# Causal attention core: looks at the heads spread over twelve of sixteen steps, hyperbolic heads three steps apart

## The reference, cut to what matters

```python
def _sdpa(q, k, v, scale):
    scores = jnp.einsum('bhtd,bhsd->bhts', q, k) * scale + _causal_bias(...)
    return jnp.einsum('bhts,bhsd->bhtd', jax.nn.softmax(scores, axis=-1), v)

def _hyp_attn(q, k, v, curv):
    tq = jnp.sqrt(1.0 / curv + jnp.sum(q * q, axis=-1, keepdims=True))
    tk = jnp.sqrt(1.0 / curv + jnp.sum(k * k, axis=-1, keepdims=True))
    inner = jnp.einsum('bhtd,bhsd->bhts', q, k) - tq * jnp.swapaxes(tk, -1, -2)
    arg = jnp.maximum(-curv * inner, 1.0 + 1e-07)
    dis = jnp.sqrt(1.0 / curv) * jnp.arccosh(arg)
    scores = 1.0 / (eps + dis) + _causal_bias(...)
    return jnp.einsum('bhts,bhsd->bhtd', jax.nn.softmax(scores, axis=-1), v)
```

## Time and profile before

| | us |
|---|---|
| three runs | 5957.14, 5960.48, 5983.22 (median 5960.48) |
| the profiled execution | 5973.35 |
| its span, from the first to the last instruction | 5971.3 |
| busy over the span: TensorE, VectorE, ScalarE, GpSimd | 4632.2 (78%), 3844.7 (64%), 2507.9 (42%), 597.5 (10%) |
| the core "g", from about 2490 to about 3680 | some 1190 |
| mean granted TensorE clock over the span | 0.854 |

### The profile page before, as it was taken

One profiled execution on the slowest core, in us unless ns is written; L12 is line 12 of the kernel. 1 busy time (PEld: TensorE's weight loads), 2 busy tenths in 40 slices (PEclk: granted clock), 3 DMA queues, 4 the chain that ended last, 5 costly groups with the idle time before them and its releaser, 6 DMA issues. The chain is left out here.

```text
span 5971.3 us, 101861 instructions
## 1 busy us (share of the span) xinstructions
PE 4632.2 (78%) x27583; PEld 3020.9 (51%) x27583; DVE 3844.7 (64%) x9327; ACT 2507.9 (42%) x5760; POOL 597.5 (10%) x928
## 2 busy tenths in 40 slices
PE   6999978850029888587787786777799899789888
PEld 5667657640015555355555554555455555444444
DVE  3444433348878878777777665555677777477776
ACT  1222224347533333377777774222366666400000
POOL 0000000000000000100000000111111111122221
PEclk9999989975569989777777777888799999899999
DMA  2111113348974444332222222555433333211110
GB/s 65 52 54 52 50 53 144 144 169 253 355 274 125 127 130 123 87 75 69 69 69 69 71 72 69 157 154 154 105 93 85 88 94 91 77 45 46 49 50 27
DMA packets 379998, 617.03 MB, mean 103 GB/s; under 512 B 43190, under 2 KB 310004, under 8 KB 379892
## 3 DMA queue, kind: packets, MB, share of 16 engines
q1 hardware_dynamic: 367572, 614.35, 35.1%
q0 software_dynamic: 12320, 1.40, 0.2%
HBM read 345.02 MB, written 269.21 MB: 103 GB/s over the span
## 5 line engine op out<-in xcount | busy, mean ns | idle before, releaser
L1645 DVE TENSOR_REDUCE e_neg<-ps 91x1 f32<-91x273 f32 x1536 | 571.9, 427 | 137.4 <-PE ps L1466 130.0
L1578 ACT ACTIVATE e_probT<-ps 91x273 f32<-91x273 f32 x1536 | 491.7, 393 | 292.9 <-PE ps L1466 292.2
L1193 PE MATMUL ps<-k_downT,f_o 128*91 128x256 f32 x1152 | 260.1, 385 | 453.6 <-DVE f_o L1101 453.4
L2320 PE MATMUL ps<-m_we,m_xT 128*128 128x512 f32 x1104 | 521.6, 621 | 0.0
L1193 PEld LDWEIGHTS ps<-k_downT,f_o 128*91 128x91 f32 x1152 | 183.0, 161 | 522.4 <-issue 454.6
L1464 PE MATMUL ps<-c_mask_kq,c_identb 91*91 91x91 bf16 x1536 | 325.8, 243 | 104.4 <-ACT g_probT L1578 79.4
L1466 PE MATMUL ps<-e_k,e_q 96*91 96x273 bf16 x1536 | 344.0, 307 | 64.9 <-DMA e_k<-s_parts 28.8
L2254 DVE SCALAR_TENSOR_TENSOR m_acc<-ps,m_weight,m_acc 128x256 f32<-128x256 f32 x552 | 261.7, 481 | 173.6 <-PE ps L2320 163.7
L1466 PE MATMUL ps<-g_q,g_k 102*91 102x273 bf16 (+5 forms) x1536 | 331.0, 296 | 49.1 <-DVEq L1651 48.5
L2320 PEld LDWEIGHTS ps<-m_we,m_xT 128*128 128x128 f32 x1104 | 211.4, 198 | 223.3 <-issue 208.9
L1466 PE MATMUL ps<-e_q,e_k 128*91 128x273 bf16 x1536 | 286.7, 291 | 38.3 <-DMA e_q<-e_shift 36.4
(11 more groups left out here) (303 smaller groups left out, 10057.6 us busy)
## 6 DMA issues: line engine op xcount, KB each, us to landing
s_gate<-b_gu SPq DMA_DIRECT2D x32, 819.0 KB
s_up<-b_gu SPq DMA_DIRECT2D x32, 819.0 KB
c_g<-s_gate SPq DMA_DIRECT2D x32, 819.0 KB, 7.0
s_gated<-c_g SPq DMA_DIRECT2D x32, 819.0 KB
d_g<-s_gated SPq DMA_DIRECT2D x32, 819.0 KB, 10.4
d_u<-s_up SPq DMA_DIRECT2D x32, 819.0 KB
s_o<-d_o SPq DMA_DIRECT2D x32, 819.0 KB
f_o<-s_o SPq DMA_DIRECT2D x32, 819.0 KB
```

Of the source, the lines that this page charges most:

```text
L1193: last = nc.tensor.matmul(ps[0:R, t // 2, (t % 2) * D:(t % 2 + 1) * D], o[:, u, k, t * R:(t + 1) * R], downT[:, k, :], start=(k == 0), sto ...
L1578: nc.scalar.activation(probT[0:R, p % 8, b, :], src, ACT.Exp, scale=float(HD) ** 0.5 if kinds[h] == COS else 1.0)\
L1645: last = nc.vector.tensor_reduce(neg[:, u, t, h:h + 1], src, AX.X, ALU.max, negate=True)
L2320: last = nc.tensor.matmul(ps[0:R, EBANK[m % 4], :], xT[:, u, k, t * R:(t + 1) * R], we[:, k, 2 * p:2 * p + 2, :].rearrange("p e d -> p (e ...
```

## The change

In the core "g" the steps of the looks are given by a table. Before, ten looks stood at steps -11 to -2, hyperbolic and SDPA heads in turn (6, 0, 7, 1, 8, 2, 9, 3, 4, 5). Now they stand from -15 to -4: hyperbolic heads 8, 9, 6, 7 at -15, -12, -9, -6 and SDPA heads 0 to 5 at -11, -10, -8, -7, -5, -4. Root, sum and score keep their distance from the look. The negation moves from step 0 (p = 0) to step -1 (p = 15), the shift's turn from step 1 to step 0. Since heads are no longer looked at in the order of their numbers, the counts that the waits compare with go by the place in the order (`z`). The extra dimensions are loaded with each half for its own two hyperbolic heads.

```diff
-        LOADS = {0: 2 * len(RUNS) + (2 if hd > HD else 0), 1: 2 * len(RUNS)}
+        LOADS = 2 * len(RUNS) + (2 if hd > HD else 0)
...
-        first = -11 if n_hyp else -13
-        look_order = [h for pair in zip(HYPS, SDPAS) for h in pair] + SDPAS[n_hyp:]
-        look_step = {h: first + x for x, h in enumerate(look_order)}
+        if n_hyp:
+            look_step = {8: -15, 9: -12, 6: -9, 7: -6, 0: -11, 1: -10, 2: -8, 3: -7, 4: -5, 5: -4}
+        else:
+            look_step = {h: h - 13 for h in range(H)}
+        look_order = sorted(look_step, key=look_step.get)
         look = {place(step): h for h, step in look_step.items()}
+        looked_hyps = [h for h in look_order if h in HYPS]
...
-            NEGATE = place(look_step[HYPS[-1]] + SCORE + 1)
-            shifts = [(look_step[HYPS[-1]] + SCORE + 2, 0, MAXED)]
+            last_hyp = max(look_step[h] for h in HYPS)
+            NEGATE = place(last_hyp + SCORE + 1)
+            shifts = [(last_hyp + SCORE + 2, 0, MAXED)]
...
-                    if hd > HD and half == 0:
-                        sp.dma_start(dst[SLOTS * HD:rows, u, HYPS[0]:HYPS[0] + n_hyp], extra_dram[n, x])\
+                    if hd > HD:
+                        own = slice(max(HYPS[0], heads.start), min(HYPS[-1] + 1, heads.stop))
+                        sp.dma_start(dst[SLOTS * HD:rows, u, own],
+                                     extra_dram[n, x, :, own.start - HYPS[0]:own.stop - HYPS[0]])\
                             .then_inc(qk_loaded[u][half], 16)
...
-                    ways = 4 + max([g for g in back_step if back_step[g] - H < shifts[x][0]], default=-1)
+                    ways = 4 + max([g for g in back_step if back_step[g] - H <= shifts[x][0]], default=-1)
                     pe.wait_ge(S["out"].sem, S["out"].at((n[0], n[1] - 1), ways - 3))
...
-                for a, h in enumerate(HYPS):
+                for h in looked_hyps:
+                    a, z = HYPS.index(h), looked_hyps.index(h)
                     if (when, p) == place(look_step[h] + ROOT):
-                        act.wait_ge(S["hu"].sem, S["hu"].at(n, a + 1))
+                        act.wait_ge(S["hu"].sem, S["hu"].at(n, z + 1))
```

More of the change, by code:

```diff
@@ L1502, in step @@
                         if h == [x for x in look_order if x // HALF == half][0]:
-                            pe.wait_ge(qk_loaded[u][half], 16 * LOADS[half] * (i + 1))
+                            pe.wait_ge(qk_loaded[u][half], 16 * LOADS * (i + 1))
                     for which in (("max", "raw") if kinds[h] == HYP else ("max",)):
@@ L1585, in step @@
                     nc.scalar.copy(oT[:, g % 2], ps[:, 6, 0:T]).then_inc(S["oT"].sem, 1)
[L1586 removed]
+                for h in looked_hyps:
+                    a, z = HYPS.index(h), looked_hyps.index(h)
                     if (when, p) == place(look_step[h] + ROOT):
[L1588 removed]
+                        act.wait_ge(S["hu"].sem, S["hu"].at(n, z + 1))
                         nc.scalar.activation(hu[:, a], hu[:, a], ACT.Ln).then_inc(S["hl"].sem, 1)
[L1590 removed]
+                        act.wait_ge(S["hl"].sem, S["hl"].at(n, z + 1))
                         nc.scalar.activation(hu[:, a], hu[:, a], ACT.Exp, scale=0.5).then_inc(S["root"].sem, 1)
                     if (when, p) == place(look_step[h] + SCORE):
[L1593 removed]
+                        act.wait_ge(S["z"].sem, S["z"].at(n, z + 1))
                         nc.scalar.activation(hw[:, u, a], hw[:, u, a], ACT.Ln, bias=one[:]).then_inc(S["l1"].sem, 1)
[L1595 removed]
+                        act.wait_ge(S["l1"].sem, S["l1"].at(n, z + 1))
                         nc.scalar.activation(hw[:, u, a], hw[:, u, a], ACT.Ln, bias=eps6[:],
                                              scale=root_ic[:, a:a + 1]).then_inc(S["l2"].sem, 1)
[L1598 removed]
+                        act.wait_ge(S["l2"].sem, S["l2"].at(n, z + 1))
                         nc.scalar.activation(hw[:, u, a], hw[:, u, a], ACT.Exp, scale=-1.0)\
@@ L1626, in step @@
                         dve.wait_ge(S["s"].sem, S["s"].at(n, y + 1))
-                        dve.wait_ge(S["score"].sem, S["score"].at(n, a + 1))
+                        dve.wait_ge(S["score"].sem, S["score"].at(n, looked_hyps.index(ORDER[p]) + 1))
                         d = hw[:, u, a, b * T:(b + 1) * T]
@@ L1633, in step @@
                     a = HYPS.index(h) if kinds[h] == HYP else None
+                    z = looked_hyps.index(h) if kinds[h] == HYP else None
                     if a is not None:
@@ L1649, in step @@
                         else:
-                            dve.wait_ge(S["top"].sem, S["top"].at(n, a * NT + (1 if b == 0 else NT)))
+                            dve.wait_ge(S["top"].sem, S["top"].at(n, z * NT + (1 if b == 0 else NT)))
                             dve.sem_inc(S["looked"].sem, 1)
@@ L1660, in step @@
                                 .then_inc(S["looked"].sem, 1)
-                        dve.wait_ge(S["w"].sem, S["w"].at(n, a + 1))
+                        dve.wait_ge(S["w"].sem, S["w"].at(n, z + 1))
                         dve.wait_ge(S["looked"].sem, S["looked"].at(n, y + 1))
@@ L1665, in step @@
                             .then_inc(S["wc"].sem, 1)
-                        dve.wait_ge(S["z"].sem, S["z"].at(n, a + 1 - n_hyp))
-                        dve.wait_ge(S["wc"].sem, S["wc"].at(n, a + 1))
+                        dve.wait_ge(S["z"].sem, S["z"].at((n[0], n[1] - 1), z + 1))
+                        dve.wait_ge(S["wc"].sem, S["wc"].at(n, z + 1))
                         nc.vector.scalar_tensor_tensor(out=hu[:, a], in0=hw[:, u, a], scalar=2.0,
@@ L1671, in step @@
                             .then_inc(S["hu"].sem, 1)
-                for a, h in enumerate(HYPS):
+                for h in looked_hyps:
+                    a, z = HYPS.index(h), looked_hyps.index(h)
                     if (when, p) == place(look_step[h] + SUM):
-                        dve.wait_ge(S["root"].sem, S["root"].at(n, a + 1))
+                        dve.wait_ge(S["root"].sem, S["root"].at(n, z + 1))
                         nc.vector.tensor_tensor(hw[:, u, a], hw[:, u, a], hu[:, a], ALU.add).then_inc(S["z"].sem, 1)
```

4 lines of the change are left out of this document (removed).

## The result

The changed kernel takes 6199.52 us (median of 4 runs, 6181.94 to 6210.76); the kernel before 5971.85 (4 runs, 5957.14 to 5989.06). The ratio is 1.0377, 95% interval 1.0334 to 1.0421: slower, by some 225 us. The forecast was 6093 with an upper end of 6145. The direction was right, and the loss was 1.7 times the 133 us that I had worked out.

A forecast was written before the change was run, and what follows sets the result against it. No engine is full; waits in the fixed order set 36.4 us a batch. Walked 21.0 + 12.8 + 5.4 = 39.2, clock +1.3: 40.5; 31 periods +127, start +6, from the 5960.48 median: 6093 us, range 6020 to 6145.

The forecast's parts named there:

- (b'): Stretch of a batch from the fourth hyperbolic look to the exponentials of step 15: 12.8 us, against 8.6 before.
- (c'): Stretch from the exponentials of step 15 to the next batch's first hyperbolic look: 5.4 us, against 9.1 before.
- look 1 to look 2: Gap between first and second hyperbolic looks: 6.8 us, through a root on ScalarE, step 3's exponentials and a TensorE product.
- Look 2 to 3: Gap between second and third hyperbolic looks, VectorE's own work: 7.2 us.
- the clock term: TensorE's lower clock level adds 1.3 us to the walked 39.2 us period, giving 40.5; upper end +2.2, 41.4.
- look 3 to 4: Gap between third and fourth hyperbolic looks, summed from VectorE's pieces: 7.0 us.
- Start: Head 8 is first, so the first look waits for the half loaded second: 3 to 4 us, prologue looks 2; +6.
- DMAs: Two more loads per batch on SP, for the extra rows in two pieces per operand: cost nothing.
- laid: Last part of the shift stands behind the first look; TensorE's wait at step 6: nothing, or up to 1 us a batch.
- ScalarE idle some 3 us before the first root: Sign expected in the new trace: ScalarE idle there, then filled from the fourth look's end to step 15.
- The rival of a low clock throughout: TensorE's clock at the lower level throughout, 42 us a period with the shift's wait: 6140 us, chance 0.10.
- That interleaving wins: Rival: spreading the looks fills VectorE's busy and idle stretches, period 32 us, 5824 us; chance 0.10.

The follow-up runs named there:

- The score one step later: The changed kernel with every score five steps behind its look instead of four, negation and shift moving one step with it; 6032.87 us, 1.0083 of the kernel before.
- head 7 sooner: The changed kernel with head 7 in the main pass at step 10 instead of 11, and head 5 at 11; 6110.66 us, 1.0217 of the kernel before.
- the kernel with 36 fillers: The changed kernel with 36 idle matmuls a batch on TensorE, placed where it waits for exponentials; 6168.43 us, 1.0313 of the kernel before.
- the old steps: The changed kernel with the looks back at their earlier steps, split loads and new counts kept; 5978.23 us, 0.9992 of the kernel before.

## Why the prediction was right in direction and short in size

**The walk was right.** At the higher clock level it gave 12.8 for (b'), 5.4 for (c') and 6.8 from look 1 to look 2; the batch with the clock at 1.00 has 12.90, 5.17 and 6.8. Look 2 to 3 was given 7.2 and is 7.16 (mean), at either level. The score one step later and head 7 sooner, which take two of its terms away, gave back 5.2 and 2.9 us of the 6.7, with some clock and jump in it, as said above.

**The step that failed is the clock term**, "so I take +1.3: 40.5 us", and with it the bound "some +2.2 us, so 41.4 is the upper end". Means over the 30 periods:

| stretch | walked, higher level | measured mean | more |
|---|---|---|---|
| (b') fourth look to exponentials of step 15 | 12.8 | 13.7 | 0.9 |
| (c') to the next first look | 5.4 | 7.3 | 1.9 |
| look 1 to 2 | 6.8 | 7.65 | 0.85 |
| look 2 to 3 | 7.2 | 7.2 | 0 |
| look 3 to 4 | 7.0 | 7.4 | 0.4 |
| sum | 39.2 | 43.3 | 4.1 |

Two things were wrong in it. First, I counted TensorE's pieces on the path only in (c') and from look 1 to 2. For these two stretches the bound was right in size: 1.3 + 0.85 = 2.15 us measured (though the pieces that it names add up to 1.9, with the durations of both levels from the rows above and in the earlier trace rows: 0.94 for the two products, 0.39, 0.22 and 0.31). But TensorE's pieces lie in (b') as well, between ScalarE's pairs of exponentials, where the lower level costs 1.0 us (13.92 against 12.90). The changed kernel shows this by itself: in six batches (b') is 12.9, in 23 it is 13.9. One of the six:

```profile
2732.11:2745.02 12.91, 7.51 (x74) 4.86 (x71) 6.58 (x20) 8.34 (x19) 0.00 (x0) 0.87 0.07 19
```

And a (c') at 1.00 in the kernel with 36 fillers, 5.17 us, where others there have 6.85 at 0.50:

```profile
2908.02:2913.19 5.17, 3.38 (x41) 2.17 (x41) 1.11 (x5) 2.27 (x8) 0.00 (x0) 1.00 0.52 115
```

Second, I took a mixture of levels, about half of the bound; in the trace look 1 to 2 is at 0.50 in 29 of 30 batches and (c') in 22. That makes 0.9 + 1.3 + 0.85 + 0.4 = 3.4 us of clock where 1.3 was taken and 2.2 was the bound. (The 1.3 of (c') is 1.9 less the jump below. That the 0.4 of look 3 to 4 is the clock is less sure: the mean clock there is 0.66, and the three shortest, 6.99 us, have 0.76, 1.00 and 0.76, but another at 0.76 has 7.13.) I had the cause in hand, TensorE standing still 2.3, 2.3 and 3.5 us inside (b') (1.96, 1.61 and 2.52 in the batch shown), and sized its effect by the mean clock of before instead of asking what level would hold in the stretch right behind the stalls.

**A term was missing.** VectorE's jump back behind the negation that waits for the last score: 1.6 us in 13 of the 31 periods, some 0.65 in the mean, which is the rest of (c')'s 1.9. Nothing in the forecast's text looks at where the loop's end falls. Before, the negation was at step 0, past it.

3.4 - 1.3 = 2.1 and 0.65 of jump, on 40.5, give 43.2 us against the 43.1 between negations. These 2.7 us, 31 times, are 84; the forecast's +127 fell short of 208 by 81. The median of 6199.52 is 106 above the 6093. 76 of these are the profiled execution's (81 of the periods, less 5 of start and end). 13 are what I had taken off because the median of three lay under the profiled one; with the fourth run it is 5971.85, only 1.5 under. 17.6 are what the changed kernel's profiled execution lies under its own median. Of the last two no trace tells more than that executions spread so.

The other points:
- Start. +6 was given. The first look's load wait is 34.97 us against the 29.96 of the earlier trace rows, +5.0 where 3 to 4 was allowed, and the first negation follows the load 26.3 us later instead of 24.5, +1.8 where 2 was. The other 3.2 of its 10 us lie ahead of the core, which the change doesn't touch.
- DMAs: nothing, shown by the old steps.
- laid: nothing. TensorE's waits for the shift's rows add up to under 3 us in the whole core.
- "ScalarE idle some 3 us before the first root" was wrong in form: it waits 2.00 us before the copy of oT and 0.66 before the root (which begins at 3015.53, 3.7 us after the look, as forecast). The rest is filled by work that I had put elsewhere.
- The turn waits for `g_out`, and the scores wait more for `g_probT`, both as forecast.
- The rival of a low clock throughout had its mechanism right and the price short for the same reason: 42 us a period for what is 43.1. That interleaving wins is refuted for this order of steps: VectorE is 177 us busy of 300 instead of 210. The Trainium skill (Perfetto Trace Analysis, Optimization Strategy) says that interleaving may help, not that it does, and here a look of 3.6 us had come to stand in front of additions that ScalarE needed.

## What to carry to other kernels

In a fixed order on several engines, spreading a heavy piece evenly puts it in front of other engines' needs: look at what each piece stands ahead of, and at two long pieces that meet in one step, before looking at how full the engines are. Where TensorE waits in the new order, price all its work behind and between the waits at the lower clock level and make that the bound, not a mean of the two; and don't buy the clock back with idle matmuls before the order is right, least of all right behind a loop's end. Find where the loop's end falls for each engine, and keep a wait that is released late from standing right before it.
